# Raw tiles issued by ScalarE from the third pair on, and the quadrants of the blocks in the order 0, 2, 1, 3

## The reference

```python
# stage 0, on x and y transposed to (positions, channels); scale = 16 ** -0.5
def xca(q, k, v):                        # per head, attention between channels
    attn = softmax(einsum('bhni,bhnj->bhij', q, k) * scale)
    return einsum('bhnd,bhde->bhne', v, attn)
res_p2r = xca(x @ wq_rgb.T, y @ wk_point.T, y @ wv_point.T) @ proj_p2r.T
res_r2p = xca(y @ wq_point.T, x @ wk_rgb.T, x @ wv_rgb.T) @ proj_r2p.T
s = (x + res_p2r) + (y + res_r2p)        # the input x of stage 1
# stage 1, s and y as (channels, positions)
q, k, v = Wq y + bq, Wk y + bk, Wv s + bv
# (the call passes s as x and y as y)
attn = softmax(q kᵀ / sqrt(128))         # per head
o = Wo (attn v) + bo + s
out = (o - mean(o)) / sqrt(var(o) + 1e-5) * gn_w + gn_b   # mean, var over a whole sample
```

## Time and profile before

| | |
|---|---|
| median of 3 runs | 327.62 us (327.05 to 328.21) |
| profiled execution, its time | 328.15 us |
| its span, first to last instruction | 326.3 us |
| TensorE busy | 307.2 us (94%) |
| VectorE, ScalarE, GpSimd busy | 261.7, 233.1, 190.1 us |
| DMA, mean over the span | 226 GB/s, 73.87 MB |
| loads on SyncE's queue (q1) | 58.92 MB, 66.7% of 16 engines' span |
| stores on ScalarE's queue (q10) | 14.68 MB, 12.9% |
| mean granted TensorE clock | 0.995 |

### The profile page before, as it was taken

One profiled execution on the slowest core, in us unless ns is written; L12 is line 12 of the kernel. 1 busy time (PEld: TensorE's weight loads), 2 busy tenths in 40 slices (PEclk: granted clock), 3 DMA queues, 4 the chain that ended last, 5 costly groups with the idle time before them and its releaser, 6 DMA issues.

```text
span 326.3 us, 12574 instructions
## 1 busy us (share of the span) xinstructions
PE 307.2 (94%) x4792; PEld 269.2 (82%) x4792; DVE 261.7 (80%) x707; ACT 233.1 (71%) x385; POOL 190.1 (58%) x277
## 2 busy tenths in 40 slices
PE   6999958999997899999999999999999999999990
PEld 4887857898986689898988989898988889898760
DVE  2495874988898498888889888888889898876883
ACT  2664734887878379787878779787878779787575
POOL 0874481675656647575766757575766746575611
PEclk9999999999999999999999999999999999999997
DMA  7999999179798985979899897979799895220036
GB/s 230 378 250 273 256 292 262 24 262 278 197 294 217 292 210 147 311 216 289 227 300 249 241 304 193 310 200 298 221 298 249 248 266 152 106 109 20 2 129 257
DMA packets 39060, 73.87 MB, mean 226 GB/s; under 512 B 4608, under 2 KB 26368, under 8 KB 39040
## 3 DMA queue, kind: packets, MB, share of 16 engines
q1 hardware_dynamic: 35008, 58.92, 66.7%
q10 hardware_dynamic: 4032, 14.68, 12.9%
HBM read 56.81 MB, written 16.78 MB: 226 GB/s over the span
## 4 chain that ended last, share of the span: by engine, by line
PE 91%; issue 3%; DVE 2%; DMA 1%; ACT 1%; SPq 0%; POOLq 0%; POOL 0%
PE oacc L427 10%; PE oacc L434 9%; PE oacc L428 8%; PE mid L530 4%; PE gacc L387 4%; PE mid L507 4%; PE mid L454 4%; PE stat L389 4%; PE tpx L344 4%; PE gacc L388 3%; PE gacc L389 3%; PE stat L387 3%; PE stat L388 3%; PE mid L516 2%; PE gacc L405 2%
## 5 line engine op out<-in xcount | busy, mean ns | idle before, releaser
L1135 POOL TENSOR_TENSOR xy_lo<-raw,xy_hi 128x256 fp32r<-128x256 f32 x256 | 179.5, 738 | 119.8 <-ACT xy_hi L704 119.8
L704 ACT ACTIVATE xy_hi<-raw 128x1024 fp32r<-128x1024 f32 x64 | 67.0, 1048 | 0.0
L866 DVE STREAM_TRANSPOSE t<-y_blocks 128x512 f32<-128x512 f32 x56 | 62.4, 1158 | 0.0
L711 ACT ACTIVATE res<-oacc 128x512 f32<-128x512 f32 x59 | 34.9, 593 | 29.0 <-PE oacc L434 28.7
L895 DVE BATCH_NORM_STATS2 hstat<-res 128x6 f32<-128x512 f32 x60 | 40.1, 687 | 15.5 <-ACT res L711 15.4
L427 PE MATMUL oacc<-xy_hi,pq_hi 128*128 128x512 f32 x120 | 52.4, 436 | 0.1
L428 PE MATMUL oacc<-xy_lo,pq_hi 128*128 128x512 f32 x120 | 47.4, 395 | 1.6 <-issue 1.6
L387 PE MATMUL gacc<-t 128*32 128x129 f32 x224 | 43.1, 273 | 2.6 <-issue 2.6
L390 PE MATMUL gacc<-t 128*32 128x225 f32 x224 | 45.4, 354 | 0.0
L389 PE MATMUL gacc<-t 128*32 128x225 f32 x224 | 45.4, 354 | 0.0
L390 PE MATMUL stat<-t 128*32 128x225 f32 x224 | 45.1, 353 | 0.0
(11 more groups left out here) (166 smaller groups left out, 905.3 us busy)
## 6 DMA issues: line engine op xcount, KB each, us to landing
raw<-in_x SPq DMA_DIRECT2D x31, 512.0 KB, 5.8
raw<-in_ctx SPq DMA_DIRECT2D x31, 512.0 KB, 6.9
y_blocks<-in_ctx SPq DMA_DIRECT2D x112, 128.0 KB, 7.0
out<-res ACTq DMA_DIRECT2D x28, 512.0 KB, 3.5
x_blocks<-in_x SPq DMA_DIRECT2D x56, 128.0 KB, 6.9
out<-res SPq DMA_DIRECT2D x4, 512.0 KB, 2.7
wt<-in_weights SPq DMA_DIRECT2D x1, 896.0 KB, 6.8
raw<-in_x SPq DMA_DIRECT2D x2, 256.0 KB, 3.8
```

Of the source, the lines that this page charges most:

```text
L704: act.activation(xy_hi[slot][:, s, :], raw[slot][:, s, :], ACT.Copy).then_inc(split_hi, 1)
L866: dve.transpose(dst, blocks[:, HC * i:HC * (i + 1)]).then_inc(yt_ready, 1)
L1135: piece = pool.tensor_tensor(xy_lo[slot][:, s, cols], raw[slot][:, s, cols], xy_hi[slot][:, s, cols].bitcast(f32), ALU.subtract)
```

## The change

The functions `raw_free` and `refill_raw` leave SyncE's program. ScalarE gets a `refill_raw` with the same waits and the same two loads. In SyncE's step only the two `refill_blocks` remain. In ScalarE's step the loads for item 0 of the pair before stand after `gram_out(p, 0)` and those for item 1 after `z_out(p - 1)`; with them pair p + 1 is loaded in step p. In step (0,1) it issues the four loads of the third pair after `u12_out`. The last step with loads is (7,0), so ScalarE's loop ends one pass sooner and (7,0) and (7,1) are straight code, as on VectorE. The loads of the first two pairs stay with SyncE. The four quadrants of a set of blocks are issued in the order 0, 2, 1, 3 in place of 0, 1, 2, 3.

```diff
+        QUAD_ORDER = (0, 2, 1, 3)
...
-                for a in range(QUADS):
+                for a in QUAD_ORDER:
                     sp.dma_start(y_blocks[n][W32 * a:W32 * (a + 1), :, :], blocks[a]).then_inc(blocks_in[n], 16)
...
-            def refill_raw(h, u, b):
-                raw_free(h, u, b)
-                load_x(h + 1, 2 * u + b)
-                load_y(h + 1, 2 * u + b)
...
             def step(h, u):
                 refill_blocks(h, u, 0)
-                refill_raw(h - 1 + u, 1 - u, 1)
                 refill_blocks(h, u, 1)
-                refill_raw(h, u, 0)
-
-            refill_raw(0, 0, 0)
+
             load_blocks(1, 2)
-            refill_raw(0, 0, 1)
             load_blocks(1, 3)
             load_x_blocks(1, 1)
-            refill_raw(0, 1, 0)
...
-            refill_raw(last - 1, 1, 1)
...
+            def refill_raw(h, u, b):
+
+                slot = 2 * u + b
+                n = 4 * h + slot
+                act.wait_ge(split_hi, 2 * n + 2)
+                act.wait_ge(split_lo, 2 * n + 2)
+                if isinstance(n, int) and n < 4:
+                    act.wait_ge(y_early_done, 2 * n + 2)
+                    act.wait_ge(x_transposed[b], n - b + 2)
+                elif b == 0:
+                    act.wait_ge(x_transposed[0], n + 2)
+                act.dma_start(raw[slot][:, 0, :], x[4 * (h + 1) + slot]).then_inc(x_in[slot], 16)
+                act.dma_start(raw[slot][:, 1, :], y[4 * (h + 1) + slot]).then_inc(y_in[slot], 16)
...
                     u12_out(p - 1)
+                    refill_raw(0, 0, 0)
+                    refill_raw(0, 0, 1)
                     xt_out(h, u, 1, 0)
...
                     gram_out(p, 0)
+                    if ahead:
+                        refill_raw(h - 1 + u, 1 - u, 0)
                     split_high(h, u, 0, 1, back)
                     gram_out(p, 1)
                     z_out(p - 1)
+                    if ahead:
+                        refill_raw(h - 1 + u, 1 - u, 1)
                     out_to_sbuf(h - 1, u, 1, 0)
...
-            steps(act, step)
+            last = PAIRS // 2 - 1
+            step(0, 0, True, False, False, False)
+            step(0, 1, True, True, False, False)
+            step(1, 0, True, True, True, False)
+            step(1, 1, True, True, True, True)
+            with act.Fori(2, last) as i:
+                step(i, 0, True, True, True, True)
+                step(i, 1, True, True, True, True)
+            step(last, 0, True, True, True, True)
+            step(last, 1, True, True, True, True, ahead=False)
+            step(last + 1, 0, False, True, True, True)
+            step(last + 1, 1, False, False, True, True)
```

More of the change, by code:

```diff
@@ L731, in store, with step @@
                 act.dma_start(out[q], res[2 * u + b][:, :]).then_inc(stored[2 * u + b], 16)
-            def step(h, u, front, middle, back, post):
+            def step(h, u, front, middle, back, post, ahead=True):
                 p = 2 * h + u
```

## The result

| | before | changed |
|---|---|---|
| median | 327.91 us (6 runs) | 334.81 us (332.90 to 335.58, 6 runs) |
| ratio of the changed kernel to before | | 1.023, 95% interval 1.017 to 1.029 |
| profiled execution, its time | 328.15 us | 335.55 us |
| its span | 326.3 us | 333.7 us |

The change makes the kernel 2.3% slower. The forecast was 341 us with a range of 330 to 353. The direction and the place of the loss in a steady step are as forecast, and its size nearly. In the profiled execution the total is smaller because the idle pieces of TensorE's first passes, which I had left as they were, went away. Some executions are over 1.5% longer than the fastest of the same kernel; the medians include them, the ratios don't, and the profiles of experiments 4 and 5 are of such executions and are read only for what is waited for.

A forecast was written before the change was run, and what follows sets the result against it. TensorE was taken to bound the kernel, with ScalarE's chain just as tight. 328.15 us plus 11 x (0.9 + 0.3) = 13.2 gave 341.35 for the profiled execution, forecast as 341 us (median 0.5 lower), range 330 to 353.

The forecast's parts named there:

- TensorE and ScalarE are equally tight: Steady step: TensorE busy throughout its 18.35 us; ScalarE's chain to the z copies has about 0.03 us of slack.
- 0.9 us a step from the issues of item 0: Between first Gram copy and split: two issues, 0.34 and 0.45, plus 0.11 for waits and registers, delay z and TensorE.
- The bound of 1.3 for both: Upper bound, in us a step, for item 0's two issues if the second is stretched to 0.69.
- 0.3 us a step from the issues of item 1: After z_out: 0.45 us visible beside the second z copy, less 0.15 of slack at N's weight load; bounds 0 and 0.8.
- 11 steps, 13.2 us: Of 13 steps with loads, (1,0) to (7,0), 11 pay 0.9 + 0.3 us each.
- The two steps that I took out: Steps (1,0) and (2,1), costed at nothing because TensorE's idle pieces there would cover the delay; otherwise 2 x 1.2 us.
- x just arrives: First transposition of a step: raw x needed 5.7 us after its issue, median landing 5.5; cost 0, 1.2 us at 7.0.
- the rival's mechanism: x lands late at each step's first transposition: 2.2 us in 12 steps, 26 us, 354 us in all; chance 0.18.
- First passes unchanged: TensorE's four idle pieces in first passes through code, 7.47 us together, were left as they were, at no gain.
- The rival: Faster: idle pieces are waits for code, up to 7.47 us back; with free issues 321 us; chance 0.10.
- The order of the quadrants costs nothing and gains nothing: Block loads in order 0, 2, 1, 3: one semaphore, consumer waits for all four; cost 0, bounds plus or minus 0.
- The four loads in (0,1), and ScalarE's longer straight code: Start: some 1.8 us of issues, cost 0, bounds 0 and 2; straight code of (7,0), (7,1): 0, bounds 0 and 2.6.

The follow-up runs named there:

- experiment 4: Kernel before with quadrants 0, 2, 1, 3 and SyncE asking for raw tiles after the step's blocks and first Gram copy; 334.90 us, ratio 1.013.
- experiment 5: Changed kernel with item 0's loads moved from behind the first Gram copy to behind z_out, ahead of item 1's; 334.50 us, ratio 1.023.
- experiment 3: Changed kernel with ScalarE's loads of item 0 moved ahead of norm_scale, where it waits for GpSimd; item 1's stay after z_out; 326.10 us, ratio 1.000.
- the repeated execution: The changed kernel, unchanged, profiled a second time; 332.95 us.
- experiment 6: Changed kernel with only item 0's y load moved behind z_out, x staying behind the first Gram copy; 332.89 us, ratio 1.015.
- experiment 11: Kernel before with quadrants 0, 2, 1, 3, item 2's raw loads later, and four unneeded 512 KB copies on SyncE's queue; 325.83 us, ratio 0.997.
- experiment 8: Kernel before with item 2's raw loads moved from ahead of SyncE's loop to behind the first blocks of step (1,0); 325.78 us, ratio 1.000.

## Why the prediction was right, point by point

- *TensorE and ScalarE are equally tight.* Right. The slack of 0.03 us at the product with z was the key reading: what was added to ScalarE between the first Gram copy and z came out of TensorE, in the place that was named, and with it gone (experiment 3) the steps are back at 18.35 us.
- *0.9 us a step from the issues of item 0.* Right in mechanism, low in size: ScalarE's idle time is 1.11 us in the mean (13.3 in 12), in the repeated execution 0.95, and without the late x the eleven steps grow by about 1.25 us each, in the repeated one by 1.0. The term that was mis-sized is the second issue, 0.45 in the sum and 0.70 to 0.86 measured, where its upper bound was 0.69. The bound of 1.3 for both was also added up wrongly: with the second issue at 0.69 the sum is 0.34 + 0.69 + 0.11 = 1.14.
- *0.3 us a step from the issues of item 1.* Wrong. They cost nothing (experiment 3 keeps them, with steps of 18.35 us). I had let the sequencer start on them a few tenths after the second z copy began; it ran ahead by four instructions and issued them beside the split. My reading of why item 0's issues get no such lead: just ahead of them stands the store at 202.21, which needs the normalisation that ends at 202.04, so the sequencer can't be further ahead than that. No run moves the store to test it.
- *11 steps, 13.2 us.* Measured 15.3 in the profiled execution and 11.6 in the repeated one. The 15.3 contain one late x of 1.59 us. The two steps that I took out were not covered: in (2,1) the pieces went, and TensorE waits 0.77 us for z there as elsewhere.
- *x just arrives.* Right. Item 0's x in steps (1,1) to (6,1) landed after 5.1 to 7.8 us, median 6.0, and the next transposition started 6.4 us after the issue in the median (6.2 in the repeated execution); two waits, 1.8 us in all. Both sides were forecast lower, 5.5 and 5.7. Experiments 4 to 6 show that it was right for the reason given: only the delayed step saves x, and the rival's mechanism is real as soon as ScalarE's delay is taken out.
- *First passes unchanged.* This is the step that failed. The forecast gave them zero and named their going as a rival, and as a sign of being wrong; in the profiled execution they gave back 7.6 us in steps (1,0) and (2,1), in the repeated one 2.0. The rival assumed cheap issues besides; its first half came true with dear ones. Its mechanism, waits for code, is the one that experiment 11 and the traces show. (Its 321 us takes off 6.5 us where its own pieces add up to 7.47; that would be 320.) Of the 4.8 us of (1,0) part is the draw of the first profile, since the kernel before has no pieces there in the second.
- *The order of the quadrants costs nothing and gains nothing.* Wrong for the kernel before, where alone it is worth 1.1%; nothing measurable within the changed one. I looked at the consumer, which waits for all four, and not at the time that the transfers take from the engines.
- *The four loads in (0,1), and ScalarE's longer straight code.* No cost is seen: the changed kernel reaches step (1,0) at 32.3 us, before 32.6.

The profiled execution was forecast at 341.35 us and took 335.55. The issues of item 0 cost 13.7 us in the eleven steps where 9.9 were forecast, those of item 1 nothing where it was 3.3, and x 1.6 where it was nothing, together 2.1 more; the first passes gave back 7.6, and an earlier start 0.3. So the total came out near the forecast partly because errors of both signs offset each other.

## What to carry to other kernels

A share of 71% says nothing of an engine's slack: compare the end of its last copy with the start of what waits for it, and put DMA issues where the engine waits anyway or where its sequencer runs ahead, never between short instructions of a full stretch. Moving a load's issue has two prices, the issuer's time and the times at which the queue is full; in this kernel, in straight code and in the first pass of the loop, a full queue stopped TensorE although no data was late. When an idle piece has no shown wait, look for an instruction transfer that ends just before it does. Profile the kernel before twice, since an idle piece that comes and goes between executions can be mistaken for an effect of an edit.

## What was not expected of the hardware

- The second of two 512 KB loads issued by ScalarE shortly after a store took 0.56 to 1.6 us to issue in steps (1,1) to (7,0) of the changed kernel (0.93 in the step shown), against 0.35 to 0.37 for the first of the two. In ScalarE's wait for rstd in experiment 3 the same load took 0.39 to 0.46. What stretches it is open.
- Loading the same blocks in the order 0, 2, 1, 3 lowered the queue's share of the DMA engines from 66.7% to 63.8% at the same 58.92 MB.
- Each of the 21 idle pieces of TensorE without a shown wait ended 1.2 to 1.6 us after the end of a 16 KB instruction transfer.
- What an idle piece costs besides itself varies. After pieces of 2.45, 2.30 and 2.24 us (experiments 3, 11 and 8) the granted clock was 0.92 to 0.93 over the step, full speed with a stretch at 1.2 GHz in it, and the step grew by 4.3 to 4.6 us. After the piece of 2.61 us in the kernel before, and after waits for x of 2.06 and 1.99 us in experiments 6 and 4, it stayed at 1.00; in experiment 5 it fell to 1.2 GHz in or just after waits of 2.13, 1.92 and 1.68.
